# Attention and a mixture of experts in one kernel: how TensorE learns which expert's weights a slot uses

## What is computed

```python
q = (x @ Wq) as 32 heads of 16;  k, v = 8 groups of 16, each used by 4 heads
weights = softmax(causal(q @ k.T) / 4);  attention = (weights @ v) @ Wo + bo
scores = sigmoid(x @ gate_w.T) + bias
topk_w, topk_idx = top_k(scores, 4)          # of 16 experts, weights made to sum to 1
z = silu(x @ Wg[e].T) * (x @ Wu[e].T)        # 256 wide, per expert
out = sum over the 4 chosen of w_e * (z @ Wd[e].T)  +  the same with a shared expert
```

## Time and profile before

| | us |
|---|---|
| median of 3 runs | 577.28 |
| the runs | 577.28, 583.11, 577.28 |
| the profiled execution | 577.56 |
| its span (first instruction to last) | 575.7 |
| TensorE busy, matmuls | 466.4 |
| VectorE busy | 372.6 |
| ScalarE busy | 260.5 |
| GpSimd busy | 258.7 |

### The profile page before, as it was taken

The page is one execution under the profiler, slowest core; times in us unless marked ns, Lnnn a source line. Parts: engine busy times, 40 slices in busy tenths (PEclk is TensorE's granted clock), DMA queues, the critical chain, the costliest instruction groups (busy, mean ns, idle before and its releaser), DMA issues.

```text
span 575.7 us, 10261 instructions
## 1 busy us (share of the span) xinstructions
PE 466.4 (81%) x2984; PEld 344.4 (60%) x2984; DVE 372.6 (65%) x656; ACT 260.5 (45%) x385; POOL 258.7 (45%) x224
## 2 busy tenths in 40 slices
PE   0993669778998987989978779997888889889970
PEld 0882458556775765567756555775666557667640
DVE  7189975847885767268879872787764536766520
ACT  1441111146555454365577542656646335545610
POOL 3000392045554543365555863555567326464410
PEclk9996889969998998989999899999989999899986
DMA  7813943255575477665778964549655534424222
GB/s 281 323 46 81 235 177 111 92 190 173 100 140 167 75 143 221 111 160 99 145 236 208 273 139 68 148 116 213 205 110 98 103 56 75 74 44 88 38 38 36
DMA packets 32861, 78.25 MB, mean 136 GB/s; under 512 B 4320, under 2 KB 12000, under 8 KB 29600
## 3 DMA queue, kind: packets, MB, share of 16 engines
q0 software_dynamic: 11936, 27.53, 26.2%
q1 hardware_dynamic: 13904, 41.60, 22.2%
q10 hardware_dynamic: 6960, 8.39, 6.8%
HBM read 54.04 MB, written 23.33 MB: 134 GB/s over the span
## 4 chain that ended last, share of the span: by engine, by line
PE 49%; DVE 19%; issue 13%; ACTq 7%; ACT 6%; DMA 2%; POOL 2%; DVEq 1%; POOLq 0%; SPq 0%
PE psum L1047 27%; PE psum L1174 5%; DVE negm L867 3%; PE psum L1184 3%; PE psum L1140 3%; ACT wsplit L516 3%; PE psum L1008 3%; PE psum L1156 2%; PE psum L1071 2%; PE psum L1057 2%; ACTq L252 1%; ACTq L250 1%; DMA xn<-x 1%; PE psum L1076 1%; PE psum L1142 1%
## 5 line engine op out<-in xcount | busy, mean ns | idle before, releaser
L1047 PE MATMUL psum<-wsplit,xgT 128*128 (+1 forms) x660 | 178.8, 422 | 9.2 <-DVE xgT L752 9.2
L1047 PEld LDWEIGHTS psum<-wsplit,xgT 128*128 128x128 f32 x660 | 128.4, 201 | 38.2 <-issue 10.1
L421 POOL DMA_INDIRECT out<-ysb,tab x48 | 89.3, 1860 | 113.3 <-ACT ysb L549 99.5
L1047 PE MATMUL psum<-wsplit,zT 128*128 (+1 forms) x336 | 95.4, 421 | 20.1 <-DVE zT L859 20.1
L1047 PEld LDWEIGHTS psum<-wsplit,zT 128*128 128x128 f32 x336 | 62.3, 196 | 38.7 <-issue 27.0
L401 POOL DMA_INDIRECT xg<-xn_rows,tab x47 | 53.1, 1129 | 39.6 <-PE psum L1184 22.1
L503 ACT ACTIVATE th<-psum 128x256 f32<-128x256 f32 x55 | 21.2, 385 | 97.5 <-PE psum L1047 94.7
L426 POOL TENSOR_TENSOR wsplit<-wraw,wsplit (+1 forms) x16 | 40.1, 2507 | 54.2 <-ACT wsplit L516 51.9
L590 ACT ACTIVATE xn<-psum 128x1536 f32<-128x1536 f32 x32 | 46.4, 1450 | 37.0 <-PE psum L1142 37.0
L934 DVE TENSOR_TENSOR plo<-xn,phi 128x1536 f16<-128x1536 f32 x32 | 59.5, 1859 | 1.1 <-DVE ctxs L945 0.2
L907 DVE TENSOR_TENSOR xgT<-psum,xgT 128x512 fp32r<-128x512 f32 x47 | 32.3, 688 | 43.0 <-ACT xgT L512 40.9
(11 more groups left out here) (174 smaller groups left out, 637.5 us busy)
## 6 DMA issues: line engine op xcount, KB each, us to landing
wraw<-wexp SPq DMA_DIRECT2D x17, 1024.0 KB
wraw<-wexp SPq DMA_DIRECT2D x17, 512.0 KB, 4.5
q_parts<-stage ACTq DMA_DIRECT2D x12, 192.0 KB
q_pack<-q_parts ACTq DMA_DIRECT2D x6, 384.0 KB
xn<-x SPq DMA_DIRECT2D x4, 512.0 KB, 5.2
xn_rows<-xn SPq DMA_DIRECT2D x8, 256.0 KB, 7.7
ctxs<-x SPq DMA_DIRECT2D x8, 256.0 KB, 4.9
out<-ysb SPq DMA_DIRECT2D x8, 256.0 KB, 3.2
```

The source lines that it names most:

```text
L421: nc.gpsimd.indirect_dma_start(out=out, out_offset=rows_of(s), in_=ysb[:, par, :], in_offset=None, compute_op=ALU.add).then_inc(y_out[par] ...
L1047: last = MM(dst, lhs(a, k), split_weights(place, w, c), start=m == 0, stop=m == len(products) - 1)
```

## The change

TensorE reads only the number of a slot. The place is worked out from it as (number + 1) % 2, which is the expert's index and 1. The read for the next slot stands behind the gate/up products of a slot, for as long as there is a next slot in the sequence; at the head of a sequence the read for its first slot stands in front of the scores. `prev` is handed from one sequence to the next, where it was read again. The other engines are as before.

```diff
--- before.py
+++ after.py
@@ -1189,14 +1189,15 @@
             pe.wait_ge(v_ready, 1)
             pe.wait_ge(shared_done, NT)
 
-            def sequence(b, last):
+            def sequence(b, last, before):
                 s0 = SPS * b
 
                 def expert_of(s):
-                    return (pe.value_load(where[0:1, 0, s + 1:s + 2], min_val=0, max_val=1),
-                            pe.value_load(where[0:1, 1, s + 1:s + 2], min_val=1, max_val=NE))
-
-                prev = expert_of(s0 - 1)
+                    number = pe.value_load(where[0:1, 1, s + 1:s + 2], min_val=1, max_val=NE)
+                    return (number + 1) % 2, number
+
+                prev = expert_of(s0 - 1) if b == 0 else before
+                ahead = expert_of(s0)
                 for g in range(G):
                     scores(b, g, G * b + (min(g + 4, G) if last else g + 4))
                     if g < QF and not last:
@@ -1204,8 +1205,7 @@
                     for j in BESIDE[g]:
                         s, first = s0 + j, j == BESIDE[g][0]
                         real = not (last and j == SPS - 1)
-                        if real:
-                            place, number = expert_of(s)
+                        place, number = ahead
                         if not (last and j + 1 >= SPS - 1):
                             rows_transpose(s + 1, 1 - j % 2, 8 * SPS * b + 16 * ((j + 1) // 2 + 1))
                         pe.wait_ge(y_sb, s + 1)
@@ -1216,6 +1216,8 @@
                             pe.wait_ge(w_low[0], 2 * number)
                             pe.wait_ge(xt_sb, s + 1)
                             gate_up(j % 2, place)
+                            if j < SPS - (2 if last else 1):
+                                ahead = expert_of(s + 1)
                         if first and not (last and g >= 4):
                             pe.wait_ge(exp_done, G * b + g + 2)
                             half = 1 - g // 4
@@ -1233,9 +1235,11 @@
                         if real:
                             prev = place, number
                 output_projection(b, 2 * b + (2 if last else 3))
-
+                return prev
+
+            before = None
             for b in range(B):
-                sequence(b, b == B - 1)
+                before = sequence(b, b == B - 1, before)
 
 
 def kernel(**inputs):
```

## The result

The changed kernel takes 575.4 us (median of 20 runs, 570.7 to 579.6) where the kernel before, run beside it, takes 580.6 (20 runs, 575.8 to 585.6). The ratio is 0.9933, with a 95% interval of 0.9904 to 0.9962: about 3.9 us faster. A second set gave 0.9925 [0.9895, 0.9954]. Together that is 4.1 us, where I had forecast 7.0. These ratios, unlike the medians, leave out the runs more than 1.5% above the fastest of their kernel, which here are more of the kernel before than of the changed one, so they lean against the change. Where I write "over all runs", the ratio is that of the plain means: over all runs the two sets give 0.9922 and 0.9906, 4.5 and 5.4 us, each uncertain by 1.3 to 1.7. The three runs shown of before (577.28) had been low for this kernel: 3.3 of the 5.1 us between the 570.3 of the forecast and the 575.4 measured are that.

A forecast was written before the change was run, and what follows sets the result against it. Bound by TensorE's order of work with pauses in it, now and then by VectorE. Sequences one to four give 2.6 + 1.2 + 0.35 + 2.85 = 7.0 us; 577.3 - 7.0 = 570.3 us, range 564.5 to 576.5.

The forecast's parts named there:

- The pause and its cause: In front of the row transposes (L1184): two register reads make 19.2 us of "issue" in 27 pieces.
- How far the sequencer gets ahead: Behind the weighted products (L1156): 17 matmuls ahead, 0.4 us of cover against 1.3 for two reads, leaving 0.9.
- One value and the parity cost nothing: Behind gate/up: read (0.65 us) and parity (0.2, bounds zero and 0.4) hidden by 2.2 us of cover.
- The signs: L1184 issue under 3 us, 48 loads, zT up 4 to 8, ysb and negm a few, no issue before L1071 or down.
- as the rival had it: Head of every gate/up group: parity costs up to 0.19 us in 47 slots, 8.9 at most; 577 us, chance 0.06.
- The clock: Six slow gate/up groups, some 1.4 us each: taken as zero, plus or minus 2.8; as rival 564.7 us, chance 0.07.
- What survives of 23.5 us: Of the 23.5 us ceiling from 27 pauses, 15 pauses on the chain that ended last give 7.0 us.
- terms for sequences two and three: 1.2 us survive in sequence two and 0.35 in three, where VectorE is busy and takes back the rest.
- The chain stays on TensorE: Sequence one: the chain stays on TensorE through its pauses, so nearly all survives, together 2.6 us.
- through TensorE alone: Argument against the other-waits rival (chance 0.18): in sequences one and four the chain runs through TensorE alone.
- The lower bound of the sum: 3.5 us gained if VectorE and ScalarE take back all but sequence four and the first pause of one and two.
- the time goes into other waits: Rival: time closed at L1184 reopens as waits for zT, ysb or negm; gain 0 to 4, 575.3 us, chance 0.18.

The follow-up runs named there:

- before: The kernel before, without the change: 580.6 us beside the changed kernel; the profiled execution took 577.56 us, a second profiled one (before_again) 583.6 us.
- one_front: Against the changed kernel: one value and its parity, read at the old place in front of the row transposes; ratio to the kernel before 0.9926.
- two_late: Against the changed kernel: both values, place and number, read behind the gate/up products, no parity; ratio to the kernel before 0.992.
- lean: Changed kernel without the second wait for the split rows (L1217) where the transposes had already waited; ratio 0.9873, repeated (lean_again) 0.9955.
- after: The changed kernel, whole change against the kernel before: 575.4 us, ratio 0.9933; run again with a profile (after_again), 0.9925.
- late_2_3_again: Second run of the kernel with the change in sequences two and three only, the others as before: ratio 1.0037, the first time 1.0055.
- lean2: Changed kernel without either wait for the split rows (L1182 in all slots but the first, and L1217): ratio to the kernel before 0.9978.
- three_front: Kernel before with a third value (the number twice) read in front of the row transposes: ratio 1.019, 11 us slower.

## Why the prediction was right, and where it was wrong

The lengths of the sequences, from the first scores to the output projection, can be compared over the traces, since each kernel has every sequence either as before or as changed. The number of traces stands in brackets.

| sequence | as before, us | as changed, us | difference | forecast |
|---|---|---|---|---|
| one | 105.7 (6), 103.7 to 107.2 | 103.1 (4), 102.4 to 103.9 | -2.6 | -2.6 |
| two | 118.2 (5), 116.3 to 120.4 | 116.7 (5), 116.0 to 117.1 | -1.5 | -1.2 |
| three | 113.0 (5), 111.4 to 114.5 | 114.8 (5), 113.0 to 116.1 | +1.7 | -0.35 |
| four | 95.9 (6), 95.0 to 97.1 | 93.2 (4), 92.0 to 94.3 | -2.8 | -2.85 |

Each difference is uncertain by about 0.7 (one standard error, the scatter over the root of the number of traces). They add to -5.2; the ratios say -4.1, over all runs -5.0. One and four together give -5.4 (forecast -5.45), two and three +0.2 (forecast -1.55). That one and four agree to 0.1 is luck at this scatter.

- *The pause and its cause: right.* The reads in front of L1184 make it; with them behind gate/up none is left.
- *How far the sequencer gets ahead: right.* A rule of the Trainium skill (Advanced Engine Details and Errata, Engine Queue Depths) gives TensorE's queue a depth of 64, with the remark that tiling complicates it; 17 matmuls with their weight loads are 34. By the rule (an estimate from its 64) one_front would have had no pause at all behind the down and weighted products, and it kept 2.2 us, all of it there. The trace disagrees with the rule, and the measurement decides.
- *One value and the parity cost nothing: nearly.* The read is hidden (two are, in two_late); the parity took 0.05 us a slot and not 0.1 to 0.4. What I costed at nothing and isn't is the head of gate/up, 2.3 us in all; lean took 2.0 of it away and gained nothing sure, so no run shows it as a cost on the path.
- *The signs: right but for size.* 48 loads; zT + 7.9 us (expected 4 to 8); ysb + 4.8 and negm + 3.9 (I said "a few"); no "issue" before L1071 or the down products. The parity stood at the gate/up group's head as the rival had it, without its price: 0.05.
- *The clock: within what was left for it.* Gate/up groups of over 3.3 us: six and four in the two traces of before, five and one in the two of after. Between them they bear no gain and no loss of mine out. They do explain scatter: after and after_again differ by four such groups of 1.5 us each or so, and by 4.6 us in their spans.
- *What failed is the step "What survives of 23.5 us", in its terms for sequences two and three.* I took the chain of the kernel before, asked at which pauses it stands, and let 1.2 + 0.35 = 1.55 us through there. Measured is nothing: 0.2 us longer by the lengths, 2.7 lost by the ratios, 1.3 lost over all runs. The next path was so close that it took over at once. Summing the chain's pieces in these two sequences shows it: in four traces as before (before, before_again and the two with the change in one and four) TensorE has 112, 109, 106 and 100 us of the chain, in four as changed (after, after_again and the two with the change in two and three) 86, 86, 89 and 91. What it gave up went to ScalarE and its queue (49 before, 60 after, means of four), to VectorE (28, 32) and to "issue" (29, 32). In these sequences I had asked this only of VectorE.
- *"The chain stays on TensorE" was not right for sequences one and four either.* In sequence one TensorE has 55 to 58 us of the chain in the traces as before and 51 in those as changed, VectorE 15 to 17 and then 17 to 20; in sequence four TensorE has 66 to 72 and then 63 to 69. So other engines took over there as well, and by less; that my terms came out is in part luck. The rival's "through TensorE alone" has the same fault: before, VectorE and ScalarE have some 30 of the 105 us of sequence one.
- *The lower bound of the sum doesn't come out of its terms.* Sequence four and the first pauses of one and two are 2.85 + 0.97 + 0.8 = 4.6, not 3.5. The 4.1 of the ratios lies between the two. The last pause of sequence four, called whole, was entered at 0.15 where it is 0.28 and 0.16 of overlap; that moves the sum by 0.3.

ScalarE's part can be read at one slot. This is the chain of after, 421 to 429 us: start us, us, what.

```profile
421.54 1.59 POOL out L421
423.13 2.54 POOL xn L410 x2
425.69 0.29 ACT phi L596
...
427.08 0.68 ACT ysb L549
...
427.80 0.69 PE psum L1057 x2
428.49 3.70 PE psum L1047 x11
```

GpSimd's scatter of a finished slot (L421) stands ahead of its mask (L410); ScalarE has phi (L596), which needs the mask, in its queue ahead of ysb (L549), and TensorE waits for ysb 2.31 us in front of L1057. In the kernel before the same place reads, on TensorE:

```profile
423.52 0.63 PE L1184 MATMUL psum<-ident,xg 128*128 128x128 f32 x4 [1.31 <-issue]
425.16 0.44 PE L1057 MATMUL psum<-ident,zz 128*128 128x128 f32 x2 [1.01 <-ACT ysb L549]
```

and on the chain, 419 to 427 us:

```profile
419.22 2.55 POOL out L421
421.77 1.25 POOL xn L410 x2
...
423.04 0.45 ACT phi L596
...
424.46 0.66 ACT ysb L549
...
425.16 0.44 PE psum L1057 x2
```

A pause of 1.31 us and a wait of 1.01: 2.3 us together, as much as the one wait of after. The chain of before goes round this pause by way of GpSimd and ScalarE, and closing it gives nothing; I had counted the wait for ysb as small because it came to 4.0 us in the whole kernel. The next view is TensorE's waits from 230 us to 456, in late_2_3_again, then from 232 to 460 in before_again:

```profile
PE psum L1047 <- DVE zT L859: 11.3, 10, 2.0
PE psum L1057 <- ACT ysb L549: 6.2, 7, 2.2
```

```profile
PE psum L1184 <- issue: 9.5, 13, 1.3
PE psum L1047 <- DVE zT L859: 7.0, 7, 1.5
PE psum L1057 <- ACT ysb L549: 3.9, 4, 1.7
```

Here 9.5 us of pause go, and 6.6 of it are at these two waits. This explains why two and three gain little. Whether sequence three grows at all is open: 1.7 us longer by the table, but lean and lean_again, changed throughout, have 111.2 and 112.7 us for it, lean2 115.1, while two and three together take 231 to 232 us in all three, between the 229.1 and 233.9 of before and before_again. It isn't that work changed places: each engine keeps the order of its program, and GpSimd has L421 ahead of L410 in both kernels. What differs in the two views is when they start and how long they take (2.54 us for the two masks against 1.25 on the chain). No run changed the order on GpSimd or on ScalarE, so that their queues set the next path is read from these rows and not tested.

Of the rivals, "the time goes into other waits" described what happened in two and three. Its gain was 0 to 4 and the forecast's own 4 to 11; 4.1 by the ratios and 5.0 over all runs stand at the border, so the time alone doesn't choose between them. I had rated it at 0.18 because I priced each wait by its total before the change, and a total says nothing of how close behind the others stand.

## What to carry to other kernels

A pause on the chain is worth, when closed, no more than the lead of its engine over the next path at that place (in sequences two and three here: nothing of 1.55 us): look there at the neighbouring engines' queues (what is ahead of the instruction that releases the next wait), not at the wait's total in the whole kernel. Lengthen a pause and it may pass 60%, shorten it and some 20%, so an experiment in the harmless direction doesn't size a gain. Where executions scatter by half a per cent, compare stages over several traces and repeat a good draw before believing it.

## What the runs showed of the hardware that I had not expected

- The parity of a register value needed no instruction of its own: the step went into an existing FUSED_REGOPS, 104 ns where before none took over 60, once for each gate/up group.
- The slowest TENSOR_LOAD took 1465 ns after (1464 in two_late) and 927 before, with a median of 302 to 305.
- Reads in front of the very first scores stand open in every kernel: TensorE is idle there for 1.1 us with one value (one_front), 2.0 to 2.2 with two (before, after), 2.8 with three (three_front) and 3.8 with four (two_late). The lengths of the sequences don't contain this pause, and no run moved these reads further ahead.
- The kernel's time scatters by about 0.5% either way, and the part ahead of the first scores by itself takes 122 to 125 us in traces whose code there is the same.
